# Fused attention and LoRA feed-forward block: transposed x normalised on VectorE with spread statistics, LoRA rows transposed one tile later

## What is computed

```python
x = L0_attn_x                      # (2, 1024, 512), float32
xn = _layernorm(x, axis=-1)        # (x - mean) / sqrt(var + 1e-5)

# attention, linear, per head
Q = elu(xn @ wq.T + bq) + 1
K = elu(xn @ wk.T + bk) + 1
V = xn @ wv.T + bv
KV = einsum('bhsd,bhse->bhde', K, V)
out = einsum('bhsd,bhde->bhse', Q, KV) / (einsum('bhsd,bhd->bhs', Q, K.sum(-2))[..., None] + 1e-8)
attn = out @ wo.T + bo

# feed-forward with a shared LoRA and 8 expert LoRAs of rank 8, the top 2 chosen by a router
w    = weights of the top 2 experts, from sigmoid(xn @ W_router)
gate = xn @ W_gate + lora(xn) + expert_lora(xn, w)
up   = xn @ W_up   + lora(xn) + expert_lora(xn, w)
hidden = silu(gate) * up
ffn = hidden @ W_down + lora(hidden) + expert_lora(hidden, w)
return x + attn + ffn
```

## Time and profile before

| what | value |
|---|---|
| median of 3 runs | 667.39 us (666.99 to 667.65) |
| profiled execution | 667.35 us, its span 665.6 us |
| TensorE matmul busy | 656.5 us, 99% of the span |
| VectorE busy | 376.3 us, 57% |
| ScalarE busy | 259.3 us, 39% |
| GpSimd busy | 127.3 us, 19% |
| chain that ended last | TensorE 94%, VectorE 4%, DMA 1% |
| slice of the span in 40, each 16.6 us, VectorE busy, tenths | 6677888779685954… in the first 16 slices |

### The profile page before, as it was taken

One profiled execution on the slowest core, in us unless ns is written; L12 is line 12 of the kernel. 1 busy time (PEld: TensorE's weight loads), 2 busy tenths in 40 slices (PEclk: granted clock), 3 DMA queues, 4 the chain that ended last, 5 costly groups with the idle time before them and its releaser, 6 DMA issues.

```text
span 665.6 us, 10324 instructions
## 1 busy us (share of the span) xinstructions
PE 656.5 (99%) x3557; PEld 544.7 (82%) x3557; DVE 376.3 (57%) x708; ACT 259.3 (39%) x419; POOL 127.3 (19%) x290
## 2 busy tenths in 40 slices
PE   7999999999999999999999999999999999999998
PEld 6889999877777788888888888888888888888886
DVE  6677888779685954433355444355344426534433
ACT  5434444476426323332243333233333324333321
POOL 3565666627336310000000000000000000000000
PEclk9999999999999999999999999999999999999999
DMA  6976665644755679940026000022400001300001
GB/s 216 312 257 210 211 241 196 251 183 158 280 197 212 233 162 3 32 174 0 0 80 247 7 0 0 0 77 76 177 0 0 0 9 70 127 0 0 0 0 63
DMA packets 41642, 74.21 MB, mean 111 GB/s; under 512 B 19392, under 2 KB 20288, under 8 KB 39952
## 3 DMA queue, kind: packets, MB, share of 16 engines
q1 hardware_dynamic: 38672, 64.52, 35.8%
q10 hardware_dynamic: 2736, 9.05, 3.4%
q0 software_dynamic: 208, 0.30, 0.3%
HBM read 52.82 MB, written 21.04 MB: 111 GB/s over the span
## 4 chain that ended last, share of the span: by engine, by line
PE 94%; DVE 4%; DMA 1%; issue 1%; ACT 1%; POOL 0%; DVEq 0%; ACTq 0%; POOLq 0%
PE bank L1268 21%; PE bank L1269 21%; PE bank L1270 21%; PE bank L1514 18%; PE bank L1487 6%; PE bank L1500 2%; PE bank L1498 1%; PE bank L1287 1%; DVE den L1108 1%; PE bank L1299 1%; DMA w_raw<-in_wkT 1%; PE bank L1525 1%; PE bank L1527 1%; PE bank L1308 0%; DVE m_l L903 0%
## 5 line engine op out<-in xcount | busy, mean ns | idle before, releaser
L1268 PE MATMUL bank<-x,up_h 128*128 128x512 f32 (+1 forms) x352 | 137.3, 390 | 0.2 <-DVE x3r L1072 0.2
L1269 PE MATMUL bank<-x,up_h 128*128 128x512 f32 (+1 forms) x352 | 137.1, 390 | 0.0
L1270 PE MATMUL bank<-x,up_l 128*128 128x512 f32 (+1 forms) x352 | 137.1, 389 | 0.0
L1205 DVE TENSOR_TENSOR hf<-bank,silu 128x512 f32<-128x512 f32 x44 | 30.4, 691 | 154.7 <-issue 135.0
L1514 PE MATMUL bank<-dn,hid_h 128*128 128x512 f32 x352 | 108.8, 390 | 0.0
L684 ACT ACTIVATE hid_h<-hf 128x512 fp32r<-128x512 f32 x44 | 27.8, 632 | 142.4 <-DVE hf L1205 142.4
L1268 PEld LDWEIGHTS bank<-x,up_h 128*128 128x128 f32 x352 | 66.1, 188 | 14.4 <-issue 0.7
L1514 PEld LDWEIGHTS bank<-dn,hid_h 128*128 128x128 f32 x352 | 65.9, 188 | 14.5 <-DVE res L1230 0.6
L1270 PEld LDWEIGHTS bank<-x,up_l 128*128 128x128 f32 x352 | 66.1, 188 | 13.8
L1269 PEld LDWEIGHTS bank<-x,up_h 128*128 128x128 f32 x352 | 66.1, 188 | 13.6
L903 DVE TENSOR_TENSOR up_l<-up_raw,up_h 128x1024 fp32r<-128x1024 f32 x44 | 53.9, 1225 | 28.0 <-ACT up_h L684 28.0
(11 more groups left out here) (170 smaller groups left out, 1083.9 us busy)
## 6 DMA issues: line engine op xcount, KB each, us to landing
x<-scr_x SPq DMA_DIRECT2D x7, 2048.0 KB, 8.6
up_raw<-in_ffn_up SPq DMA_DIRECT2D x11, 768.0 KB, 8.2
scr_x<-xt ACTq DMA_DIRECT2D x16, 512.0 KB, 5.1
xin<-in_x SPq DMA_DIRECT2D x16, 256.0 KB, 4.9
scr_z<-zt SPq DMA_DIRECT2D x16, 256.0 KB, 2.1
x3r<-in_x SPq DMA_DIRECT2D x16, 256.0 KB, 3.4
scr_att<-x3r SPq DMA_DIRECT2D x16, 256.0 KB, 3.5
z<-scr_z SPq DMA_DIRECT2D x4, 1024.0 KB, 4.9
```

The source lines that it names most:

```text
L1205: nc.vector.tensor_tensor(hf[:], ps_u[:], silu[:], ALU.mult).then_inc(h_done, 1)
L1268: nc.tensor.matmul(dst, lh, rh, start=start, stop=False, **kw)
L1269: nc.tensor.matmul(dst, lh, rl, start=False, stop=False, **kw)
L1270: return nc.tensor.matmul(dst, ll, rh, start=False, stop=stop, **kw)
```

## The change

- The input x is also given transposed (`xT`, 128 x 16 x 4 x 128), and SP loads 256 KB of it for each of tiles 2 to 15 into a new buffer `xtr` of two slots (`load_xt(t+2)`, after `xtl_done`). The loads of x wait for `ln_stats` in place of `ln_done`.
- For tiles 2 to 15 the normalised tokens are no longer transposed. TensorE spreads the mean and the deviation of each token over all partitions with two fp32 transposes (`spread_statistics`), and VectorE computes (xT - mean) * deviation with two 128x512 operations that read these from PSUM (`normalise_transposed`, between `kb` and `compare`). `normalise` is left for tiles 0 and 1.
- ScalarE's `tokens_hi` and VectorE's `tokens_lo` read `xtr` in SBUF in place of the PSUM bank. `tokens_hi` moves behind relu and exp of the keys.
- The copy `zraw` moves from VectorE to ScalarE.
- The LoRA rows of tile t-3, not t-2, are transposed in tile t, directly behind the spread statistics. `lora_lo` moves ahead of `key_values` and of the weights' subtraction, `lora_out` ahead of the weights' rounding.
- In the seam: `lora_transposed(13)` in front of keys by values, `lora_transposed(14)` behind `kv_transposed(1)`; `lora_lo(13)` on VectorE in front of `heads_of(1)`; the rounding of sa_r and sb_r on ScalarE goes behind `kvt_hi(1)`, and their subtractions on VectorE go behind `lora_lo(15)`, in front of `queries(1, (2,))`. One store of LoRA rows (tile 13) is issued by ScalarE, and `store_z(12)` goes ahead of the load `x3_load(1)`.
- The loop over tiles starts at tile 4 in place of tile 2, so two more tiles are written out.

```diff
         def tiles(eng, body):
-            body(0, 0, 0)
-            body(1, 0, 1)
-            with eng.Fori(0, SPLIT_FROM // 2 - 1) as p:
-                body(2 * p + 2, p + 1, 0)
-                body(2 * p + 3, p + 1, 1)
+            for t in range(4):
+                body(t, t // 2, t % 2)
+            with eng.Fori(2, SPLIT_FROM // 2) as p:
+                body(2 * p, p, 0)
+                body(2 * p + 1, p, 1)
...
# SP
-            def stage1(t, s, more=True):
+            def load_xt(t, s):
+                sp.dma_start(xtr[:, s:s + 1].rearrange("p o k n -> p o (k n)"),
+                             dram["xT"][:, bass.ds(t, 1)].rearrange("p o k n -> p o (k n)")).then_inc(xtr_in[s], 16)
+
+            def stage1(t, s, more=True, more_t=True):
+                if more_t:
+                    sp.wait_ge(xtl_done, t + 1)
+                    load_xt(t + 2, s)
                 if more:
-                    sp.wait_ge(ln_done, t + 2)
+                    if isinstance(t, int) and t == 0:
+                        sp.wait_ge(ln_done, 2)
+                    sp.wait_ge(ln_stats, t + 2)
                     load_x(t + 3, 1 - s)
...
             sp.wait_ge(k_ready, TILES)
+            store_z(TILES - 4)
             x3_load(1)
...
# ScalarE
             def tokens_hi(t, s, uses):
-                act.wait_ge(xt_ready, t + 1)
+                early = isinstance(t, int) and t < 2
+                act.wait_ge(xt_ready if early else ln_done, t + 1)
...
+                elif ahead(t, 1):
+                    tokens_hi(t + 1, 1 - s, half + s)
                 if ahead(t, 1):
                     store_tokens(t + 1, 1 - s)
...
+                if behind(t, 3):
+                    lora_out(t - 3)
...
+                act.wait_ge(vz_ready, t + 1)
+                if behind(t, 2):
+                    act.wait_ge(zst_done, t - 1)
+                nc.scalar.activation(zraw[:, s], ps_z, ACT.Copy).then_inc(zraw_done, 1)
...
# VectorE
+            def normalise_transposed(t, s, uses):
+                dve.wait_ge(xtr_in[s], 16 * uses)
+                dve.wait_ge(xt_ready, t + 1)
+                mean, dev = (ps_xt[:, i * P:(i + 1) * P].unsqueeze(1).to_broadcast([P, KD, P]) for i in range(2))
+                nc.vector.tensor_tensor(xtr[:, s], xtr[:, s], mean, ALU.subtract).then_inc(xc_done, 1)
+                dve.wait_ge(xc_done, t - 1)
+                nc.vector.tensor_tensor(xtr[:, s], xtr[:, s], dev, ALU.mult).then_inc(ln_done, 1)
...
                 nc.vector.tensor_tensor(kb[:], ps_k[:], bk_b[:], ALU.add).then_inc(kb_done, 1)
+                if ahead(t, 1) and not first:
+                    normalise_transposed(t + 1, 1 - s, half + s)
...
-                if ahead(t, 2):
-                    normalise(t + 2, s)
-                dve.wait_ge(vz_ready, t + 1)
-                if behind(t, 2):
-                    dve.wait_ge(zst_done, t - 1)
-                nc.vector.tensor_copy(zraw[:, s], ps_z).then_inc(zraw_done, 1)
+                if behind(t, 3):
+                    lora_lo(t - 3)
...
-                if behind(t, 2):
-                    lora_lo(t - 2)
...
             compare(TILES - 1)
             kvt_lo(0)
-            lora_weighted(TILES - 2, TILES % 2)
             select(TILES - 1)
             queries(0, (0,))
             key_values(TILES - 1, TILES // 2 - 1)
+            lora_lo(TILES - 3)
             heads_of(1)
+            lora_weighted(TILES - 2, TILES % 2)
             queries(0, (1,))
...
             kvt_lo(1)
             lora_lo(TILES - 1)
+            dve.wait_ge(shr_done, 1)
+            nc.vector.scalar_tensor_tensor(sa_r[:]…, lomask[:, 1:2], sa_dn[:]…, ALU.mult, ALU.add)
+            nc.vector.scalar_tensor_tensor(sb_r[:]…, lomask[:, 2:3], sb_dn[:], ALU.mult, ALU.add
+                                           ).then_inc(shl_done, 1)
             queries(1, (2,))
             m_lo(1, range(KD))
...
# TensorE
+            def spread_statistics(t):
+                pe.wait_ge(ln_rstd, t + 1)
+                wait(pe, xtl_done, t)
+                nc.tensor.transpose(ps_xt[:, 0:P], mv[:, 0:1].to_broadcast([P, P]), ident[:])
+                nc.tensor.transpose(ps_xt[:, P:2 * P], rstd[:].to_broadcast([P, P]), ident[:]).then_inc(xt_ready, 1)
...
                 if ahead(t, 1) and not first:
-                    transpose_tokens(t + 1)
+                    spread_statistics(t + 1)
+                if behind(t, 3):
+                    lora_transposed(t - 3)
...
             queries(0, (0,))
+            lora_transposed(TILES - 3)
             keys_by_values(TILES - 2, TILES // 2 - 1, 0)
             keys_by_values(TILES - 1, TILES // 2 - 1, 1)
             pe.wait_ge(kb_done, TILES)
             queries(0, (1,))
-            lora_transposed(TILES - 2)
             queries(0, (2,))
             kv_transposed(1)
+            lora_transposed(TILES - 2)
             queries(0, (3,))
```

More of the change, by code:

```diff
@@ L461, in _ @@
             sp.dma_start(w_raw[:, 1], dram["wqT"]).then_inc(s2_in, 16)
-            store_z(1)
+            store_z(0)
             load_dn(1)
@@ L465, in _ @@
                 stage1(2 * p + 2, 0)
-                store_z(2 * p)
+                store_z(2 * p - 1)
                 x3a_load(p)
@@ L469, in _ @@
                 stage1(2 * p + 3, 1)
-                store_z(2 * p + 1)
+                store_z(2 * p)
                 load_dn(2 * p + 1)
             for t in range(2 * GT + 2, TILES):
-                stage1(t, t % 2, more=(t + 3 < TILES))
+                stage1(t, t % 2, more=(t + 3 < TILES), more_t=(t + 2 < TILES))
                 if t < TILES - 1:
-                    store_z(t - 2)
+                    store_z(t - 3)
                 if t < FC:
@@ L486, in _ @@
             sp.dma_start(sa_dn[:], dram["sa_dn"]).then_inc(sa_in, 16)
-            for t in range(TILES - 3, TILES - 1):
-                store_z(t)
+            store_z(TILES - 2)
             def x4_load(g):
@@ L704, in stage1 @@
                 first = isinstance(t, int) and t == 0
-                if ahead(t, 1):
-                    tokens_hi(t + 1, 1 - s, half + s)
+                if first:
+                    tokens_hi(1, 1, 0)
                 act.wait_ge(kb_done, t + 1)
@@ L908, in stats_of @@
                 dve.wait_ge(bn_done, t + 1)
-                wait(dve, ln_done, t)
+                wait(dve, ln_done if isinstance(t, int) and t < 3 else xt_ready, t)
                 nc.vector.memset(spare[:], 0.0)
@@ L1156, in _ @@
             key_values(TILES - 1, TILES // 2 - 1)
+            lora_lo(TILES - 3)
             heads_of(1)
+            lora_weighted(TILES - 2, TILES % 2)
             queries(0, (1,))
-            lora_weighted(TILES - 1, (TILES - 1) % 2)
-            lora_lo(TILES - 2)
-            queries(0, (2,))
             dve.wait_ge(bdnh_done, 1)
             sub(bdn[0:ER, 1], bdn_raw[0:ER, 1], bdn[0:ER, 1]).then_inc(bdn_done, 1)
-            dve.wait_ge(shr_done, 1)
-            nc.vector.scalar_tensor_tensor(sa_r[:].rearrange("p a n -> p (a n)"), sa_r[:].rearrange("p a n -> p (a n)").bitcast(F32),
-                                           lomask[:, 1:2], sa_dn[:].rearrange("p a n -> p (a n)"), ALU.mult, ALU.add)
-            nc.vector.scalar_tensor_tensor(sb_r[:], sb_r[:].bitcast(F32), lomask[:, 2:3], sb_dn[:], ALU.mult, ALU.add
-                                           ).then_inc(shl_done, 1)
+            queries(0, (2,))
+            lora_lo(TILES - 2)
+            lora_weighted(TILES - 1, (TILES - 1) % 2)
             queries(0, (3,))
@@ L1180, in _ @@
             lora_lo(TILES - 1)
+            dve.wait_ge(shr_done, 1)
+            nc.vector.scalar_tensor_tensor(sa_r[:].rearrange("p a n -> p (a n)"), sa_r[:].rearrange("p a n -> p (a n)").bitcast(F32),
+                                           lomask[:, 1:2], sa_dn[:].rearrange("p a n -> p (a n)"), ALU.mult, ALU.add)
+            nc.vector.scalar_tensor_tensor(sb_r[:], sb_r[:].bitcast(F32), lomask[:, 2:3], sb_dn[:], ALU.mult, ALU.add
+                                           ).then_inc(shl_done, 1)
             queries(1, (2,))
```

46 lines of the change are left out of this document (25 added, 21 removed).

## The result

| | before | changed |
|---|---|---|
| median | 667.30 us (15 runs, 666.96 to 667.79) | 668.68 us (15 runs, 668.13 to 669.67) |
| profiled execution | 667.35 us, span 665.6 | 669.67 us, span 667.9 |
| VectorE busy | 376.3 us | 388.5 us |

A forecast was written before the change was run, and what follows sets the result against it. TensorE's list was taken to bound stage 1, with VectorE having least room. 667.35 - 3.2 (transposes) + 0.85 (kv_transposed(1)) + 1.8 (shared_down(1)) = 666.8 us, range 664.2 to 668.8.

The forecast's parts named there:

- Step 1: Transposes on TensorE's path, tiles 2 to 15: 0.11 us each, LoRA pair about 0.1 more; -3.2 us, pair 14.6 us.
- Rival E: Each transpose holds TensorE for its reported 0.27 us, so 28 give 7.6 us: 662.4 us; chance 0.02.
- Step 2: VectorE's list in a tile: 7.1 us, 14.5 a pair against TensorE's 14.62; it fits, nothing lost.
- the operation without a row: VectorE's new operation reading a 128-wide PSUM row four times, absent from the trace; taken at 0.683 us from the nearest row.
- step 4: Seam, shared_down(1): moved sa_r and sb_r subtractions meet GpSimd's qn_l, m_l ends late; new TensorE wait, +1.8 us.
- rival C: VectorE becomes the pace in tiles 8 to 13, meeting GpSimd's rank chain; 0.4 us a tile, 668.8 us; chance 0.15.
- step 3: kv_transposed(1): VectorE enters tile 15 late after tile 14, so TensorE waits for kvm; +0.85 us, bounds 0.3 and 1.4.
- the 3.2 of the sum: The gain from fewer transposes and the LoRA pair in the forecast's sum, 667.35 - 3.2 + 0.85 + 1.8.

The follow-up runs named there:

- LoRA behind: Changed kernel with TensorE's two LoRA transposes of tile t-3 moved behind the value products of tile t: 668.09 us.
- the last kernel: Changed kernel with sa_r/sb_r subtractions back, select behind kf (tile 14: behind heads_of(0)), LoRA transposes behind value products, first xT load left early: 665.09 us.

## Why the prediction was wrong, by its own steps

**Step 1 held.** The pair takes 14.65 us where VectorE doesn't hold it, against 14.62 forecast, and the two spreads hold TensorE for 0.22 us (93.85 to 94.07 in tile 11). Rival E, 0.27 us for each transpose, would have taken 1.1 us from a pair and has no support.

**Step 2 failed, in two places.** The first is a mis-sized term. I had VectorE's pair at 14.5 us "with 0.1 to spare"; it takes 15.18. My items add up to 7.0 a tile and 14.3 for the pair; I had written 7.1 and 14.5. Item by item, from the rows of tiles 12 and 13: kb, the two new operations and compare take 2.70 and 2.69 us (2.65 forecast), so the operation without a row was sized rightly. The wait for the rank costs 0.4 in each tile in place of 0.2. kf has 0.72 us to the next start, not 0.60, since lora_lo's first operation behind it starts only 0.03 us after its end, and so has the weights' subtraction in tile 13. That is 0.09 + 0.41 + 0.35 of the 0.88 us. The rank's part has a cause that I had in hand: I charged the meeting of VectorE and GpSimd in full in step 4, named it again in rival C, and set it aside because "12.67 busy microseconds held no such delay at the old subtraction". But the old subtraction reads PSUM; it could hold none. In TensorE's list this is why tiles 12 and 14 take 8.24 and 8.22 us instead of 7.78: 0.2 for xt and 0.3 for zt in each. The second is a wait that I left out. The LoRA transposes moved from the end of a tile to its middle, behind `zt_done` of VectorE's lora_lo. I booked 0.1 us of gain for it and did not ask who is late there. Tile 14 is where VectorE comes last, as step 3 says (heads_of(0), the rank, 1.12 us now); the first to ask for VectorE's result is not kv_transposed(1), but these transposes in tile 15. They cost 1.12 us, and 0.31 and 0.30 before.

**Step 3, right mechanism, no cost.** kvm ended at 138.90, 17.5 us into tile 15, where I had 17.3. But TensorE came at 139.18 and not at 16.5 us into the tile, because it had paid already. Where the transposes wait less (LoRA behind, 0.7 us; the last kernel, 0.5) the wait for kvm is there. The two are one debt, not two.

**Step 4 held.** 1.37 us of wait against 1.8, in the order forecast: sa_r 1.24, sb_r 1.78, the query's sum 1.77, m_l until 165.72 (165.4). It cost 0.2 us more in the stretch up to expand(1), which I had at nothing and whose cause I did not look for; it goes with the subtractions.

**The sum** since tile 1, by differences of the table: -1.94 at tile 15, +1.20 in tile 15 (1.12 of it the wait), -0.09 to kv_transposed(1), +0.19 to expand(0), +1.46 to shared_down(1), +0.23 to expand(1), +0.02 after it: 1.07 us. What is left of the 1.4 us between the medians lies in the start, or can't be seen. Among the rivals it is C, which I gave 668.8 us, "paid within the tiles", and a chance of 0.15. Its mechanism is the one that came, but that it came so close in time is partly luck. C charged 2.85 us of lateness up to kv_transposed(1), 0.85 of it there, while of the 3.0 us that the transposes give (14 tiles at half of 15.08 - 14.65) 2.2 were lost, and none of it there; the gain is 0.2 us smaller than the 3.2 of the sum, and 0.3 us of the medians, in the start or unplaced, are in none of its terms.

## What to carry to other kernels

When work goes from the engine that is the pace to one with "some room", write the receiver's list from start to start, with its waits, and take as room only what waits for the pacing engine: 0.41 us a tile put into the kernel before cost 2.3 us, although VectorE was idle 2.4 us of each pair. An operand that moves from PSUM to SBUF changes the neighbour on GpSimd too; ask the same of every instruction whose operands change, not only of those that move. And once an engine is late, its lateness is one debt that is paid at the first place where its result is asked for: moving that place (0.2 us) gives nothing, shortening its list (1.7 us) does.

## What the runs showed of the hardware

**The start is not the same each time.** Tile 1 of the kernels with the changed start began at 16.58, 16.83, 16.86, 16.87, 16.98, 17.56, 17.63 and 17.98 us. In the changed kernel's profile the key products of tile 0 were 0.43 us apart:

```profile
9.16 0.80 PE L1297 MATMUL bank<-wk_h,xt 128*128 128x512 f32 x1 [0.52 <-DVE xt L926]
9.75 0.63 PE L1298 MATMUL bank<-wk_l,xt 128*128 128x512 f32 x1
10.18 0.63 PE L1299 MATMUL bank<-wk_h,xt 128*128 128x512 f32 x1
...
13.15 0.39 PE L1297 MATMUL bank<-wk_h,xt 128*128 128x512 f32 x1
```

512 columns in 0.43 us are the 1.2 GHz level; from 13.15 on they are 0.23 apart. The views print a granted clock of 1.00 for this stretch too, but the trace's record of the clock begins only at 13.11 us, at full clock, and the views count a stretch without a record as full. So the clock rose here in the middle of the keys of tile 0. In the second profile of the same kernel the record begins at 9.91, and the products start at 9.22, 9.81, 10.09 and then 0.23 apart. In the kernel before it begins at 7.65, ahead of the keys (so its clock was not full over the whole span, as I had written, but from 7.65 us on), and all but the first are 0.23 apart. TensorE had run products with the identity matrix from 3.5 to 3.7 us on in all three, and had idled 0.52, 0.40 and 0.71 us ahead of the keys. What decides when the clock rises is open. It isn't the only cause of a late start: the profiles with tile 1 at 17.56 and 17.63 have the clock up by 8.74 and 8.15, and waits of 1.0 and 0.7 us for the value weights' va_l in tile 0. A comparison of two single profiles is thus best made from a point behind the start.

**Two SBUF inputs beside GpSimd.** In the changed kernel a 128x512 operation of VectorE on two SBUF operands took 1.77 to 1.78 us beside GpSimd's long ones, against 0.69 to 0.75 alone, and GpSimd's eq 0.78 instead of 0.32 beside VectorE's.
